# A decoder layer on one core: the feed-forward stage cut into three-part steps, its weights split earlier, and ten weight pieces loaded at the start

## The reference

```
x = layernorm(x + attention(x))        # causal, 16 query heads, 4 key/value heads of 128, rotary
x = layernorm(x + wkv(w, u, x, ctx))   # a scan over the 256 tokens, channel by channel
x = layernorm(x + ffn(x))
ffn(x):  h      = silu(x @ rw1.T + rb1)                 # 512 -> 64, the router
         logits = (h @ rw2.T + rb2)[:, :16] + gates     # 64 -> 16 experts
         coeff  = softmax over the top 2 logits, 0 for the other 14
         low    = x @ A.T                               # 512 -> 16 experts x rank 16 = 256
         out    = x @ W.T + bias + (low * coeff) @ B    # "dense" and "delta"
```

## Time and profile before

| | |
|---|---|
| median of 3 runs | 1706.19 us (1702.93 to 1711.54) |
| the profiled execution, its own time | 1708.15 us |
| its span, first to last instruction | 1706.1 us |
| busy: PE, DVE, ACT, POOL | 93%, 84%, 60%, 55% |
| mean granted clock of TensorE | 0.977 |

### The profile page before, as it was taken

How to read it: one execution, slowest core, us unless ns; L and a number is a source line. 1 busy time by engine, 2 the same in 40 slices (tenths; PEclk the granted TensorE clock), 3 DMA queues, 4 the chain that set the end, 5 groups by cost and what they waited for, 6 DMA issues and landing times.

```text
span 1706.1 us, 33011 instructions
## 1 busy us (share of the span) xinstructions
PE 1594.0 (93%) x10880; PEld 1445.9 (85%) x10880; DVE 1438.7 (84%) x3489; ACT 1026.5 (60%) x2770; POOL 930.7 (55%) x712
## 2 busy tenths in 40 slices
PE   4899999999999999999999999999999966897998
PEld 3789988989999898989998999899989855776886
DVE  2555589898989998999899899989998987989887
ACT  2777676767676767776767676767676750121111
POOL 2545566666666666666657675757575613213211
PEclk8999999999999999999999999999999987999899
DMA  6665434424442444244424442443244230211121
GB/s 223 210 241 180 132 121 137 149 57 143 143 131 57 143 143 130 56 143 143 134 63 139 154 125 69 144 154 106 81 155 143 77 115 25 84 65 50 62 75 50
DMA packets 82936, 202.73 MB, mean 119 GB/s; under 512 B 11728, under 2 KB 12240, under 8 KB 82768
## 3 DMA queue, kind: packets, MB, share of 16 engines
q1 hardware_dynamic: 82768, 200.63, 37.4%
HBM read 120.89 MB, written 37.75 MB: 93 GB/s over the span
## 4 chain that ended last, share of the span: by engine, by line
PE 68%; DVE 18%; issue 8%; ACT 4%; POOL 1%; DMA 1%; DVEq 1%; SPq 0%; POOLq 0%; ACTq 0%
PE bank L448 21%; PE bank L450 20%; PE bank L449 20%; PE bank L564 4%; DVE QS L1098 2%; DVE A L1114 1%; DVE PS L1105 1%; DVE S L963 1%; DVE PTl L952 1%; DVE Xl L1144 1%; DVE RC L979 1%; DVE ED L1118 1%; PE bank L555 1%; DVE RO L1031 1%; PE bank L547 1%
## 5 line engine op out<-in xcount | busy, mean ns | idle before, releaser
L448 PE MATMUL bank<-Xh,W 128*128 128x256 f32 x1344 | 385.6, 287 | 70.1 <-DVE RC L979 24.6
L450 PE MATMUL bank<-Xh,W 128*128 128x256 f32 x1344 | 379.9, 283 | 0.0
L449 PE MATMUL bank<-Xl,W 128*128 128x256 f32 x1344 | 378.8, 282 | 0.0
L448 PEld LDWEIGHTS bank<-Xh,W 128*128 128x128 f32 x1344 | 257.5, 192 | 80.6 <-DVE Xl L1144 28.4
L861 POOL TENSOR_TENSOR Ql<-RC,Qh 128x512 fp32r<-128x512 f32 x128 | 167.2, 1306 | 266.0 <-ACT Qh L648 266.0
L450 PEld LDWEIGHTS bank<-Xh,W 128*128 128x128 f32 x1344 | 258.8, 193 | 0.0
L449 PEld LDWEIGHTS bank<-Xl,W 128*128 128x128 f32 x1344 | 257.9, 192 | 0.0
L648 ACT ACTIVATE PTh<-bank 128x384 fp32r<-128x384 f32 x256 | 125.2, 489 | 215.1 <-PE bank L564 214.4
L663 ACT ACTIVATE S<-S,NM 128x128 f32<-128x128 f32 (+1 forms) x512 | 227.7, 446 | 41.2 <-DVE NM L963 40.6
L648 ACT ACTIVATE S<-S,RL 128x128 f32<-128x128 f32 (+1 forms) x512 | 204.3, 448 | 78.5 <-DVE RL L971 77.8
L851 POOL TENSOR_TENSOR SW<-SW,tables 128x512 f32<-128x512 f32 x128 | 168.1, 1314 | 113.7 <-DMA SW<-QB 112.6
(11 more groups left out here) (128 smaller groups left out, 4289.3 us busy)
## 6 DMA issues: line engine op xcount, KB each, us to landing
W<-kept SPq DMA_DIRECT2D x140, 512.0 KB, 4.4
SW<-QB SPq DMA_DIRECT2D x256, 128.0 KB, 2.3
kept<-W SPq DMA_DIRECT2D x40, 512.0 KB, 4.8
KVT<-in_wraw SPq DMA_DIRECT2D x40, 256.0 KB, 4.8
XR<-in_xt SPq DMA_DIRECT2D x16, 512.0 KB, 4.3
XR<-XR SPq DMA_DIRECT2D x64, 128.0 KB, 2.3
RO<-in_xn SPq DMA_DIRECT2D x16, 512.0 KB, 4.0
KVT<-in_ctxt SPq DMA_DIRECT2D x16, 512.0 KB, 4.3
```

What stands on the lines that cost most here:

```text
L448: nc.tensor.matmul(dst, lhs[0], rhs[0], start=first, stop=False)
L449: nc.tensor.matmul(dst, lhs[0], rhs[1], start=False, stop=False)
L450: return nc.tensor.matmul(dst, lhs[1], rhs[0], start=False, stop=last)
```

## The change

**Start.** There are ten staging buffers of one piece each instead of four; they lie in KVT, A2, E2 and ED, tiles of the scan that are idle until the first tail. SP issues x first, then K's pieces, two constants, four pieces, five constants, four pieces, and eight constants with a semaphore of their own (`const_more`), for which POOL waits in slot 0. The first lists of `SPLIT_AT` and `KEEP_AT` change, and `AHEAD` is 4.

**Feed-forward.** A step has three parts, and `PARTS_AT` places each part in a slot: parts of steps 0 to 2 in slots 250 to 264, steps 3 to 14 in slots 265 to 292, steps 15 to 19 behind the last slot. The ten weight pieces are split in slots 252 to 261. The router's weights are appended to those of the low-rank product, so that one group of 24 matmuls with 320 columns gives both. The hidden layer then has tokens on partitions (128 by 2 x 64); it is transposed by TensorE and copied by ACT before the logits. The bias of the logits and the gates are added to each other once, at the start. POOL makes the coefficients and weights the low-rank product; ACT applies the norm and reads the low-rank product out of PSUM.

```diff
-SPLIT_AT = [[-9, -8, -7, -6] + [h - 5 for h in range(HEADS)] + [h // 2 + 3 for h in range(HEADS)],
+SPLIT_AT = [[-7, -6, -5, -5, -3, -2, -2, -1, 0, 1, 2, 3] + [h // 2 + 4 for h in range(HEADS)],
-AHEAD = 2
+AHEAD = 4
+STAGES = 10
-FFN_WEIGHTS_AT = ALL + 1
+FFN_SPLIT_AT = [252 + i for i in range(2 * KC + ER)]
-STEPS_AT = {n: k for k, n in enumerate((264, 266, 268, 270, 271, 272, 277, 279, 281, 283, 285, 291))}
+PARTS_FROM = ALL + 9
+PARTS = [2, 1, 1, 2, 2, 1, 2, 2, 1, 1, 2, 0, 1, 2, 1, 0, 1, 1, 1, 3, 1, 1, 2, 2, 0, 1, 1, 1, 0]
...
+        stages = [a[:, 2 * i:2 * i + 2, :].rearrange("p k t -> p (k t)") for a in (KT, VT, A2, E2, ED) for i in range(2)]
...
+            load_x(0)
+            load_piece(PK)
+            load_piece(PK + 1)
+            for dst, src in FIRST_CONSTS:
+                load_const(dst, src, const_first)
+            for i in range(4):
+                load_piece(PV + i)
...
-            pool.wait_ge(const_in, 16 * len(CONSTS))
-            gp.tensor_scalar(NRb1, Rb1, -1.0, None, ALU.mult)
...
+                if part == 0:
+                        for t in range(TT):
+                            for k in range(KC):
+                                last = three(bank[2 + t][:, 0:LW], [x[:, f % 2, k, t * P:(t + 1) * P] for x in X],
+                                             [wl_tile(i, k) for i in range(2)], k == 0, k == KC - 1)
+                        pe.wait_ge(weighted, f + 1)
...
+                elif part == 1:
+                    dense(0)
+                    turn_x2(0)
+                            last = nc.tensor.transpose(bank[4][0:HID, t * P:(t + 1) * P], HE[:, t, :], Ident[:, :])
+                else:
+                    dense(1)
+                    turn_x2(1)
+                            last = nc.tensor.matmul(bank[4][:, T + a * EXP:T + (a + 1) * EXP], HST[:, a * P:(a + 1) * P], Rw2, start=True, stop=True)
+                        for t in range(TT):
+                            for r in range(ER):
+                                last = three(bank[5 + t][:, :], [a[:, r, t * P:(t + 1) * P] for a in WT],
+                                             [wd_tile(i, r) for i in range(2)], False, r == ER - 1)
```

More of the change, by code:

```diff
@@ L126, with decoder @@
             TURNS.append(("y", tail_of(n, T_Y + t), t))
[L127 to L132, removed]
+def decoder(nc, xt, xn, ctxt, wraw, bq, bk, bv, bo, wdec, ubon, wf, wl, wb, rw2,
             fbias, rb1, rb2, gates, cos_t, sin_t, mask_t, ident_t, iota_t, out):
@@ L344, in run @@
                                 splits(hf, i)
-                if ffn_weights and 0 <= n + ahead - FFN_WEIGHTS_AT < NF:
-                    ffn_weights(n + ahead - FFN_WEIGHTS_AT)
-                if n in STEPS_AT:
-                    step(STEPS_AT[n])
-            for n in range(len(STEPS_AT), STEPS):
-                step(n)
+                if ffn_weights:
+                    ffn_weights(n)
+                for k, part in PARTS_AT.get(n, []):
+                    step(k, part)
+            for n in range(FIRST_STEP_BEHIND, STEPS):
+                for part in range(3):
+                    step(n, part)
         def stage_of(n, lag):
@@ L441, in _ @@
+            for u in range(PV + 4, STAGES):
+                load_piece(u)
+            for dst, src in MORE:
+                load_const(dst, src, const_more)
             run(sp, slot, splits, ffn_weights, step, ahead=AHEAD)
@@ L565, in slot, with step @@
                     last.then_inc(turned, 1)
-            def step(n):
-                def low_rank(t):
-                    f = stage_of(n, 2)
-                    if f is not None:
-                        if t == 0:
-                            above(pe, weighted, f - 1)
-                        else:
-                            pe.wait_ge(xt_lo, TT * f + TT)
-                        for k in range(KC):
-                            last = three(bank[3 + f % 2][:, t * T:(t + 1) * T], [x[:, f % 2, k, t * P:(t + 1) * P] for x in X],
-                                         [wa_tile(i, k) for i in range(2)], k == 0, k == KC - 1)
-                        last.then_inc(low_done, 1)
+            def step(n, part):
                 def turn_x2(t):
@@ L631, in step @@
-                if f is not None:
-                    pe.wait_ge(silu_done, f + 1)
-                    above(pe, lg_b, f)
-                    for a in range(TT):
-                        last = nc.tensor.matmul(bank[2][:, T + a * EXP:T + (a + 1) * EXP], HS[:, a * P:(a + 1) * P], Rw2, start=True, stop=True)
-                    last.then_inc(logits_done, 1)
-                delta(0)
-                turn_x2(0)
-                dense(1)
-                delta(1)
-                turn_x2(1)
+                            for t in range(TT):
+                                last = nc.tensor.transpose(bank[1][:, r * T + t * P:r * T + (t + 1) * P], WX[:, t, r * P:(r + 1) * P], Ident[:, :])
```

472 lines of the change are left out of this document (272 added, 200 removed).

## The result

The changed kernel takes 1663.45 us (median of 4 runs, 1662.7 to 1666.78) against 1706.9 us (1702.93 to 1711.54) of the kernel before (4 runs): a ratio of 0.9748 [0.9727, 0.9769], 43.4 us less. The forecast was 1640 us, so the gain came out at two thirds of the 66 us that were forecast, at 1663.45 within the range of 1618 to 1670, but outside the forecast's own 1625 to 1650. The span fell from 1706.1 to 1661.6 us, by 44.5.

What follows compares the result with a forecast made beforehand. PE bounds attention and the final steps, DVE the window between. Feed-forward from 1397 plus 232, 2.9 and 14 ends PE at 1646, the kernel at 1654; with 15 from the start, about 1640 us, range 1618 to 1670, own 1625 to 1650.

Steps and rivals of the forecast that it cites:

- The three places that were to give time: The start, the DVE-bound window from 1406 to 1600.6 us, and the columns that PE streams in a feed-forward step.
- start, at slot 252: Earlier first matmul and less queueing before the attention slots: 15 us gained, bounds 4 and 20, carried through attention one for one.
- period on PE, 16 times: A feed-forward step on PE takes 14.0 us instead of 14.9, over 16 batches.
- window's loss, with the clock: Steps 3 to 14, beside the last tails: 8% of PE's 172 us lost to chains, 14 us, bounds 3 and 49.
- the 8: At the end: 8 us of PE for the last output projections and the tails' transposes, beside the 16 steps.
- some 3 of those come back: At the start, from slot 4 to slot 5: 9.6 us against a later pace of 5.3, some 3 us gained.
- 320 columns: Merged router and low-rank matmuls: 0.147 us each, between 256 and 512 columns; rival as dear as 512, +34 us, chance 0.05.
- The gap for Xl: PE's wait for Xl inside a feed-forward step goes: 0.35 of the 14.9 us.
- Weighting chain: Logits to weighted product: 5.7 us, POOL's part 2.8, under 6.3 of PE's cover; in step 18 uncovered, 2.9 us of waiting.
- Slots 252 to 256: The feed-forward's splits put 3 us on a full DVE there; counted as nothing, bounds 0 and +5 us.
- POOL and DVE in each other's way: Rival: three hold-ups lengthen the weighting chain, 1.9 us of waiting in each of 15 steps, +28, 1668 us; chance 0.12.
- The window doesn't close up: Rival: last tail's chain sets the pace, ending at 1600.6, or about 1585 with the earlier start; 1648 us, chance 0.2.

Runs made afterwards that it cites:

- experiment 1: The kernel before with only the start's edits (x first, ten staging buffers, three groups of constants, new first lists): 1696.99 us, 0.9938 of before.
- experiments 1 and 2: Each half alone; the second is the changed kernel with the start of the kernel before, feed-forward in three-part steps as changed: 1675.05 us, 0.9814 of before.
- experiments 6 and 10: 6: changed kernel, POOL comparing logits by value, no index search: 1661.73 us. 10: also splits from slot 255, step 18's half dense product before transposes: 1657.71 us.
- experiment 8: The changed kernel with DVE's reciprocals in the last two tails covering 2 of 256 columns: 1663.2 us, 0.9727 of before.
- experiment 9: The changed kernel with one cross term left out of the feed-forward's dense product, 8 of 24 matmuls a step: 1650.56 us, 0.9664 of before.
- experiment 7: Two versions of the changed kernel: feed-forward splits from slot 255 instead of 252, 1663.17 us; feed-forward's norm applied on DVE again, 1668.23 us.
- experiment 4: The changed kernel with the seven weighting operations back on DVE instead of POOL: 1680.72 us, 0.9843 of before.

## Why the prediction was right in its direction and 22 us short in size

The three places that were to give time all gave it, and the two halves of the change add up (experiments 1 and 2). The size was 22 us off, most of it in the window. The span came out 22.6 us over the forecast's 1639. By the steps:

| step | forecast | measured | adds |
|---|---|---|---|
| start, at slot 252 | -15 | -12.7 (1347.06 to 1334.32) | 2.3 |
| feed-forward begins, with the start as measured | 1384.3 | 1385.9 | 1.6 |
| period on PE, 16 times | 14.0 | 14.36 | 5.8 |
| window's loss, with the clock | 14 | 26.5 | 12.5 |
| wait in step 18 | 2.9 | 2.64 | -0.3 |
| last norm | 8.2 | 8.8 | 0.6 |
| sum | | | 22.5 |

The window's loss is what remains of 266.9 us (1385.9 to PE's end at 1652.8) less 16 x 14.36, the 8 and step 18's wait. PE's waits in the rows above are 27.1 - 2.6 = 24.5 us of it; the 2 us that are left can be the clock of 0.98: an estimate, 2% of some 200 us, gives up to 4.

- **Start: 15 forecast, 12.7 came.** The scores at 34.21 were at the edge of 31 to 34. The term that was mis-sized is the next one, "some 3 of those come back" from slot 4 to slot 5: the stretch took 8.5 us instead of 9.6, so 1.0 came back. Slots 5 to 9 then take 23.1 us where before they took 20.4, but that is made up by slot 17 (13.6 us earlier). The forecast named ACT and DVE as what could hide the gain and gave that no price; DVE's cosines stand behind splits that wait for ACT. What the forecast calls half clock the traces show as a pace: before, the matmuls of 256 columns start 0.213 us apart from 14.77 to 19.46 and 0.118 apart from 19.78 on; after, 0.214 apart from 8.27 to 10.84 and 0.114 from 11.12 on. The clock column reads 1.00 in both stretches. The 12.7 is also one of the better executions: in the nine other traces with this start slot 252 begins between 1334.6 and 1337.7, mostly near 1336.6, which is 10.4 us earlier than before, and experiment 1 measures 10.6.
- **320 columns: right.** In the low-rank product of step 16 matmuls start at 1612.85, 1612.99, 1613.14: 0.147 apart, as worked out between 256 and 512.
- **Period: 14.0 forecast, 14.36 measured; PE's own part was right by luck.** The gap for Xl that I "put at 0.35" was not there. My own row excluded it: PE was busy 89.06 of 89.4 us behind the slots, 0.06 us idle a step. But the merged product gave more than the 0.68: router and low-rank took 4.65 us with the starts of their groups (1615.64 to 1620.29), and the 24 matmuls now take 3.52 (1612.85 to 1616.37), 1.13 less. The two errors cancel: experiments 6 and 10, with the same matmuls, run at 14.08 us. The 0.28 between that and 14.36 are short stops that the forecast had at nothing: 0.25 for QB in step 15, and 0.2 for the hidden layer in step 16, which the table of waits leaves out.
- **Window: mis-sized by 12.5, the largest term.** I compared sums (PE 172, DVE 142) and took 8% for chains. The sum for DVE was short as well (158.8 measured in 199.45), but experiment 8 speaks against DVE's sum as the limit, and 4, 7 and 9 fit the queue's order and the chains to QB and to the hidden layer. Half the waits, 14.8 of 27.1 us, are for things that the forecast had no term for: the last tails' RO and KVT, the hidden layer, OTl.
- **Weighting chain: cover 6.3 forecast, slack 0.6; measured slack 0.30.** POOL took 3.27 instead of 2.8, since operations on 16 columns cost 0.42 us and not 0.25. In steps 15 to 17 that was nearly enough (0.25 us of waiting in step 15); in the window, where DVE comes later to the top 2 and POOL is held up, it was lost seven times. Experiment 9 shows the chains about 0.9 us below the step.
- **Slots 252 to 256: 0 forecast, +4 came**, within the bounds of 0 to 5, and experiment 7 shows it moves the end by little. From 252 to 260 it is 4.6 (45.7 us against 41.1), and PE's waits from 1385 to its end are 27.1 us: both just inside the limits of 5 and 30 at which the forecast called itself wrong.
- **POOL and DVE in each other's way (12%).** It happens, and in the chain that the rival named too, but not 28 us worth. In the changed kernel, step 17, all engines:

```profile
1631.79 1.29 POOL L1027 TENSOR_TENSOR KRC<-RC,Bo 128x512 f32<-128x512 f32 x1
1631.81 1.36 DVE L1274 TENSOR_SCALAR SW<-SW 128x128 f32<-128x128 f32 x1 [0.38 <-ACT SW L851]
...
1634.54 0.41 PE L665 MATMUL bank<-Ident,SW 128*64 128x128 f32 x2 [0.49 <-DVE SW L1278]
```

The same operation takes 0.23 us in the rows of experiment 4, with none of POOL's additions of 512 columns beside it. DVE is held up by 1.13 us and PE stops for 0.49; that is part of the 3.8 us for the hidden layer. The operation held up took 1.36 us, its neighbour, which starts 0.02 us before it, 1.29. The 28 us were three hold-ups a step of 0.83 us (1.00 us beside POOL's pair less 0.17 alone), less the slack of 0.6. That there would be three in every step no run shows: in steps 15 to 18 the seven POOL operations took 3.27 to 3.35 us, and in the step of the window below three of them were held up, by 1.64 us together (4.91 less 3.27).

In the window it is POOL that is held up, in the weighting chain, beside DVE's work on the last tails (a scan, and two products behind it, 1.28 us from 1506.33):

```profile
1505.10 1.30 DVE L1181 TENSOR_TENSOR_SCAN PS<-KVT,Wb 128x256 f32<-128x256 f32 x2
...
1505.91 1.23 POOL L1034 TENSOR_SCALAR S<-small,S 128x16 f32<-128x16 f32 x1
```

From its first coefficient to QB POOL takes 4.91 us in this step (1504.62 to 1509.53) instead of 3.27, and PE waits 1.23 for it. POOL's 48 operations on 16 columns take 27.9 us in the window, where 48 x 0.43 is 20.6. An estimate from the seven waits, each counted up to what its chain took over 3.27: 4.6 of the 9.7 us are this. No run takes it apart. DVE's index operations weren't held up: 32 of them took 0.17 us each.
- **The window doesn't close up (20%).** The rival has the last tail end where it did, 12.7 earlier by the start alone. Its last transposes on PE, before:

```profile
1600.37 0.60 PE L587 MATMUL bank<-Ident,RO 128*128 128x128 f32 x4
```

and after:

```profile
1583.75 0.63 PE L595 MATMUL bank<-Ident,E 128*128 128x128 f32 x4 [0.88 <-DVE RO L1235]
```

They come 16.6 us earlier. By the sign that the prediction gave, an end of the last tail at about 1585, the rival would be right; with the start as measured the sign should have been 1587.9, and the tail ended 4 us before that. The rival's price did not come: it had 62 us behind the tail's end, and there are 78 (1583.75 to 1661.6), since the whole of step 14 stands behind it too. Step 15 starts at 1598.45, where the forecast's terms give 1588 (1384.3 + 13 x 14 + 8 + 14). The tails' own waits on PE (RO and KVT) are 7.8 us of the 27.1, and 12.6 us less of their work on DVE did not shorten the window (experiment 8): the tails are a part of what holds it open, not the whole.

What stays open: how the 14.8 us of the tails' and the hidden layer's waits divide between the placement of the parts and DVE's queue. Another table of slots wasn't tried. Of the 31.8 us of the feed-forward's half, the weighting on POOL is about 16 and the norm off DVE about 4 by experiments 4 and 7; the rest, with the merged product, the three-part steps and the earlier splits, wasn't taken apart.

## What to carry to other kernels

When several chains share one in-order engine, don't price a step by that engine's busy time: ask of each chain what stands ahead of its next instruction in that queue. Moving work to an engine on which it is dearer can pay (16 us here, for operations of 0.42 us where they took 0.29, and a pair of 1.20 where it took 0.76) if it leaves the queue of a chain that is waited for. Every term needs a row; a gap that you "put" must be checked against the idle time that the profile shows, even when the sum comes out right, and a cover of 0.6 us in 6 is no cover while its parts are estimates.

## What the runs showed of the hardware

- fp32r matmuls of 320 columns start 0.147 us apart, between 0.117 (256) and 0.23 (512): in these three the cost follows the columns.
- POOL, on 16 columns with two fused operations: 0.42 us, on 32 columns 0.25, on 256 with a broadcast operand 0.60 each. The fused pair on 16 columns is dearer than the single operation on 32, which I had not expected.
- On DVE the 16-column operation takes 0.29 us, the weighted pair 0.76.
- Operations of the two engines that ran side by side were held up in both directions: DVE's on 128 columns took 0.23 us, and 1.36 beside POOL's addition of 1.29; POOL's on 16 columns took 0.42, and up to 1.23 beside DVE's work on the tails.
